# Swin-block kernel: the fifth head's queries and keys come out of the value products, and every engine's order in a step is rewritten

## The chip, the cores and the metric

One core of one Trainium2 chip runs the whole program. The metric is the device time of one execution in microseconds, the median over runs. TensorE does the matmuls, VectorE (DVE) and ScalarE (ACT) empty PSUM and do the elementwise work, GpSimd (POOL) does small side work, and SyncE (SP) issues the DMAs.

## What is computed

```
x2  = relu(x)                                  # 8 images, 16 channels, 56x56
x3  = concat(conv9x9(x2), x2) -> tokens of 160 # DIM = 160
for layer in (0, 1):                           # windows 7x7, layer 1 shifted by 3 and masked
    n   = layernorm(x3);  q,k,v = split(n @ qkvw + qkvb)     # 5 heads of 32
    a   = softmax(q @ k.T * 32**-0.5 + bias (+ mask)) @ v
    x3  = x3 + a @ projw + projb
    x3  = x3 + gelu(layernorm(x3) @ w1 + b1) @ w2 + b2       # MLP = 640
y   = x3 @ linw + linb
out = conv1x1(concat(conv9x9_transposed(y), y)) + convb
```

## The kernel before

Three phases follow each other: the first convolution (phase_a), the two Swin layers (phase_b) and the last convolutions (phase_c). The change is in phase_b alone, which works in strips of two window rows: 16 windows, 784 tokens, held as 7 tiles of 112 tokens. There are 32 strips in each of the two layers, so 64 strips.

phase_b is software-pipelined. One body handles three strips at once: the attention of strip i (`la`), the MLP of strip i-1 (`lm`), and the front of strip i+1 (`ln`): turning its normalised tokens and making Q, K and V from them. All engines run an order written out by hand, once in each engine's `body`, and meet by semaphores. A body in which all three are present is called steady. A steady body leaves out waits that the order makes unnecessary.

The names used below. Attention works on four groups j = 0..3 of four windows (two side by side, in both window rows), and the MLP and the products on two halves `HALF` of 4 and 3 tiles.

- T1 (`front_turned`): transposes of z1, the normalised input, into z1t; ACT copies them (`front_hi`) and DVE subtracts the rounded part (`front_lo`). A product of split operands is four matmuls (`split_passes`, L147).
- Q0, K0, B0 and Q1, K1, B1 (`front_product`): queries and keys of heads 0 to 3 for half a strip, 128 weight columns against 400 token columns, and B: queries and keys of the fifth head, 64 weight columns against the same 400.
- V0 to V3 (`values`): values of group j; here the tokens (114) are the stationary side and the 160 weight columns stream.
- `scores(j)`, `weights_turned(j)`, `outputs(j)`, OTj (`outputs_turned`), P0 to P2 (`projection`): attention of group j. Scores and outputs work on 64x64 tiles of the array; each is 20 fp32 matmuls that the trace shows as 40 records. The scores of two row groups go to two PSUM banks.
- T2 (`mlp_turned`), G0 to G9 (`mlp_in`), W0 to W5 (`mlp_out`; W0 has two token tiles, the others one): the MLP. L0 to L3 (`linear`): in layer 1's bodies only.

PSUM banks are shared in rotations. `RA` is a list of uses that take the three banks `ra` in turn, so its order must be the order in which TensorE fills them. `G_USES`, `L_USES` and `W_USES` name the bank of each MLP use; slot 2 is the bank `pt_ps` of the turned weights. `a_freed`, `a_room` and `m_freed` give the semaphore value at which a bank is empty.

The normalisation of a strip's input is `xa_stats` (DVE), `inv_std` (POOL), `xa_normalised` (DVE) and `repeat_rest` (POOL). SP loads the next strip into xa when `xa_normalised` is done. In the kernel before, body i does both `xa_stats(i+2)` and `xa_normalised(i+2)`, and TensorE turns the result a body later.

Of the kernel before, what the change touches and what calls it, by code (L numbers as in the profile page):

```python
# [31 lines left out]
CR = 3 * REST  # L32
# [21 lines left out]
QN = 16 * WQ  # L54
FT = MLP // 128
# [671 lines left out]
def phase_b(nc, keep, late, xs0, xs1, ys):  # L727
    with ExitStack() as ctx:
# [6 lines left out]
        def bank(name):  # L735
# [24 lines left out]
        q4, k4 = sb("q4", [128, QN]), sb("k4", [128, QN])  # L760
# [29 lines left out]
        FRONT = ["T1A0", "T1C0", "T1A1", "T1C1", "Q0", "K0", "B0", "V0", "V1", "Q1", "B1", "K1", "V2", "V3", "OT0"]  # L790
# [6 lines left out]
        T2_USES = [("T2A0", 0), ("T2C0", 1)]  # L797
        G_USES = [(f"G{g}", n) for g, n in enumerate((2, 1, 0, 2, 1, 0, 1, 2, 0, 1))]
        L_USES = [("L0", 2), ("L1", 0), ("L2", 1), ("L3", 2)]
        W_USES = [(f"W{n}", n % 2) for n in range(len(PAIRS))]  # L800
# [180 lines left out]
        def _(pool):  # L981
# [29 lines left out]
            gp.memset(q4[:], 0.0)  # L1011
# [17 lines left out]
            def body(i, la, lm, ln, more=True):  # L1029
                m = i - 1  # L1030

                def front_rest(n):
                    inv_std(n)
                    pool.wait_ge(s_norm[0], n + 1)
                    repeat_rest(z1, s_z[0])

                if lm is None and la is None:
                    front_rest(0)
                if lm is None and la is None:
                    gp.memset(vb[:], 1.0)  # L1040
                    for t in pr:
                        gp.memset(t[:], 0.0)
                    gp.tensor_copy(view(gather, 0, QP, 0, [[WT, 2], [1, WT]]),
                                   view(keep.ident, 0, QP, 0, [[WP, 2], [1, WT]]))
                    gp.tensor_copy(gather[:, GK:QP], keep.ident[0:QP, WT:WP]).then_inc(s_clear, 1)
                if more:
                    front_rest(i + 2)
# [25 lines left out]
        def _(act):  # L1073
            act_ = nc.scalar.activation

            def body(i, la, lm, ln, more=True):
                m = i - 1

                def front_hi(hf):
                    t0, nt = HALF[hf]  # L1080
                    for part, dst, rows in (("A", z1t[0], 128), ("C", z1t[2], CR)):
                        use = f"T1{part}{hf}"
                        act.wait_ge(*a_full(i, use))
                        act_(view(dst, 0, rows, t0 * WIN, [[WIN, nt], [WP, 16], [1, WIN]]),
                             view(bank_a(i, use), 0, rows, 0, [[TT, nt], [WIN, 16], [1, WIN]]), ACT.Copy).then_inc(s_hi1, 1)
# [14 lines left out]
                def fifth_head(hf):  # L1100
                    use = f"B{hf}"
                    act.wait_ge(*a_full(i, use))
                    dims = [[2 * WQ, 4], [1, WT]]
# [7 lines left out]
                def values(j, n):  # L1111
                    use = f"V{j}"
                    act.wait_ge(*a_full(n, use))
                    act_(view(vb, 0, QP, j * VJ, [[VW, 2 * HEADS], [1, HD]]),
                         view(bank_a(n, use), 0, QP, 0, [[HD, 2 * HEADS], [1, HD]]), ACT.Copy).then_inc(a_freed(n, use)[0], 1)
# [37 lines left out]
                if la is not None:  # L1153
                    weights_out(1, i)
                    values(3, m)
# [16 lines left out]
                if ln is not None:  # L1172
                    front_hi(0)
                if la is not None:
                    outputs_hi(1)
                    exps(2, i)
                if ln is not None:
                    front_hi(1)
                if la is not None:
# [8 lines left out]
                if ln is not None:  # L1188
                    values(0, i)
                    values(1, i)  # L1190
                if la is not None:
# [5 lines left out]
                if ln is not None:  # L1197
                    weights_out(0, i + 1)
                    exps(1, i + 1)
                    queries(1)  # L1200
                    fifth_head(1)
                    keys(1)
                    values(2, i)
# [5 lines left out]
        def _(dve):  # L1209
# [43 lines left out]
            def body(i, la, lm, ln, more=True):  # L1253
# [151 lines left out]
                if lm is not None:  # L1405
                    t_lo(1)
                if la is not None:
                    outputs_lo(0)
                if la is not None:
# [13 lines left out]
                if ln is not None:  # L1423
                    front_lo(1)
                if la is None and lm is None:
                    xa_stats(1)
                if lm is not None:
                    mlp_out(0)
                if more:
                    xa_normalised(i + 2)  # L1430
                if lm is not None:
                    mlp_out(1)
                    mlp_out(2)
                if la is not None:
                    outputs(2)
                if ln is not None:
                    scores_biased(0, i + 1, ln)
                    scores_max(0, i + 1)
                    scores_less_max(0, i + 1)
                if la is not None:  # L1440
                    outputs_lo(2)
                    outputs(3)
                if ln is not None:
                    scores_biased(1, i + 1, ln)
                    scores_max(1, i + 1)
                if la is not None:
                    outputs_lo(3)
                if lm is not None:
# [3 lines left out]
                if lm is not None:  # L1452
                    mlp_out(4)
                if la is not None:
# [7 lines left out]
                    residual(2)  # L1462
                    dve.wait_ge(s_pow, 2 * i + 1)
# [11 lines left out]
        def _(pe):  # L1475
            mm, tr = nc.tensor.matmul, nc.tensor.transpose

            def turn(z, hf, bank_of, room, full, name, freed_already=()):
                t0, nt = HALF[hf]
                for part, f0, rows in (("A", 0, 128), ("C", 128, CR)):  # L1480
# [8 lines left out]
            def body(i, la, lm, ln, more=True):  # L1489
# [16 lines left out]
                def front_turned(hf):  # L1506
                    if hf == 0 and not steady:
                        pe.wait_ge(s_z[0], i + 2)
                    turn(z1, hf, lambda u: bank_a(i, u), lambda u: a_room(i, u), lambda u: a_full(i, u)[0], "T1",
                         ("T1A0",) if steady else ())  # L1510

                def front_product(name, hf):
                    c0, n = {"Q": (0, 128), "K": (128, 128), "B": (256, 2 * HD)}[name]
                    use = f"{name}{hf}"
                    if use == "Q0":
                        pe.wait_ge(*a_freed(i, "T1C1"))
                    if use != "Q0" or not steady:
                        room_a(use)
                    filled_a(use, split_passes(nc, bank_a(i, use)[0:n, 0:QH], *[view(t, 0, t.shape[0], hf * 4 * WP, [[8 * WP, 2], [WP, 4], [1, WQ]])
                                                 for t in z1t],  # L1520
                                               *[w[:, c0:c0 + n] for w in keep.w["qkv", ln]], True))

                def values(j, n, l):
                    use = f"V{j}"
                    reach(pe, *a_room(n, use))
                    wv = [w[:, 2 * DIM:3 * DIM] for w in keep.w["qkv", l]]
                    for w in range(2):
                        c = slice((8 * w + 2 * j) * WP, (8 * w + 2 * j) * WP + QP + 1)
                        last = split_passes(nc, bank_a(n, use)[0:QP + 1, w * DIM:(w + 1) * DIM], *[t[:, c] for t in z1t], *wv, False)
                    last.then_inc(a_full(n, use)[0], 1)  # L1530

                def scores(j, n):
# [13 lines left out]
                    for b in range(HEADS):  # L1546
                        for row in range(2):
# [3 lines left out]
                            for w in range(2):  # L1551
                                c = j // 2 * QH + w * (4 * WQ) + (2 * (j % 2) + p) * WQ
                                q = qm[rows, h % 2 * QN + c:h % 2 * QN + c + WT] if h < 4 else q4[rows, c:c + WT]
                                k = (kt if h < 4 else k4)[rows, c:c + WT]
# [490 lines left out]
```

## Time and profile before

| | |
|---|---|
| median of 3 runs | 2950.62 us (2948.6 to 2956.58) |
| the profiled execution | 2952.52 us, span 2951.0 us, mean granted clock 0.986 |
| TensorE matmul busy | 98% of the span |
| TensorE weight loads busy | 92% |
| VectorE, ScalarE, GpSimd busy | 75%, 58%, 28% |
| DMA | 52 GB/s mean |

Ends of matmuls are modelled and overlap the next one, so a busy TensorE can hide short waits; the start of one block of matmuls to the start of the next shows what a block really took.

### The profile page before, as it was taken

How to read it: one execution, taken by the hardware profiler on the slowest of the kernel's cores; microseconds unless marked ns; L12 is line 12 of the kernel's file. 1: busy time of each engine (PE TensorE's matmuls, PEld its weight loads, DVE VectorE, ACT ScalarE, POOL GpSimd, SP SyncE). 2: the span in 40 equal slices, each digit the busy share in tenths (PEclk: the TensorE clock that was granted, in tenths of full speed). 3: DMA queues.
4: the chain of work that ended last, by engine and by line, in shares of the span. 5: the costliest groups of instructions: out<-in, count | busy, mean ns of one | idle time of the engine just before them, and what ended most of it. 6: DMA issues, size and time to landing. Idle time of an engine off the chain costs nothing. (4 is left out here: it accounts for less than half of the span.)

```text
span 2951.0 us, 94022 instructions
## 1 busy us (share of the span) xinstructions
PE 2883.9 (98%) x39898; PEld 2703.9 (92%) x39898; DVE 2213.6 (75%) x6736; ACT 1721.5 (58%) x4076; POOL 837.1 (28%) x1470
## 2 busy tenths in 40 slices
PE   8979999999999999999999999999999999999799
PEld 6669999999999999999999999999999999999799
DVE  5667777887787777787788878778878878887422
ACT  6446666666666666666656655565656555665321
POOL 8122222222222222222323322232323332332111
PEclk9969999999999999999999999999999999999899
DMA  6321111111111111111112221121111111112374
GB/s 155 128 90 25 40 46 43 46 43 46 43 43 30 42 43 46 43 46 43 46 26 47 58 58 34 33 44 44 42 24 44 44 44 25 42 43 46 65 136 77
DMA packets 210768, 152.23 MB, mean 52 GB/s; under 512 B 15954, under 2 KB 205205, under 8 KB 210331
## 3 DMA queue, kind: packets, MB, share of 16 engines
q1 hardware_dynamic: 207619, 142.41, 21.0%
q8 instruction: 308, 5.05, 0.7%
q10 hardware_dynamic: 1008, 3.44, 0.5%
q0 software_dynamic: 1728, 0.48, 0.2%
q14 instruction: 105, 0.86, 0.1%
HBM read 95.64 MB, written 52.50 MB: 50 GB/s over the span
## 5 line engine op out<-in xcount | busy, mean ns | idle before, releaser
L1627 PE MATMUL rm<-w,ht 128*112 128x160 f32 x4480 | 676.5, 300 | 0.0
L1627 PEld LDWEIGHTS rm<-w,ht 128*112 128x112 f32 x4480 | 619.7, 177 | 11.8
L1051 POOL TENSOR_TENSOR rs<-ln_tmp,mhalf 112x4 f32<-112x4 f32 (+1 forms) x128 | 118.8, 928 | 980.3 <-DVE ln_tmp L1233 980.3
L1148 ACT ACTIVATE ht<-rm 128x336 f32<-128x336 f32 (+1 forms) x448 | 216.6, 490 | 124.6 <-PE rm L147 124.5
L1091 ACT ACTIVATE qm<-ra,qpair 128x400 f32<-128x400 f32 x256 | 138.1, 590 | 214.4 <-PE ra L147 214.4
L1124 ACT ACTIVATE pt<-pt_ps 113x490 f32<-113x490 f32 x256 | 149.4, 584 | 184.7 <-PE pt_ps L1566 184.7
L1005 POOL TENSOR_TENSOR z<-z,one 112x448 f32<-112x448 f32 (+2 forms) x192 | 131.4, 684 | 358.2 <-DVE z L1237 358.2
L1119 ACT ACTIVATE pr<-sm 113x490 f32<-113x490 f32 x256 | 159.5, 623 | 88.4 <-DVE sm L1296 87.7
L1338 DVE TENSOR_TENSOR ot_lo<-ra,ot_hi 128x98 fp32r<-128x98 f32 x512 | 109.1, 255 | 128.1 <-ACT ot_rest L1131 118.0
L1131 ACT ACTIVATE ot_hi<-ra 128x98 fp32r<-128x98 f32 x512 | 102.1, 259 | 141.3 <-PE ra L1601 141.3
L1296 DVE TENSOR_TENSOR sm<-sc,mx 113x490 f32<-113x490 f32 x256 | 177.6, 694 | 6.6
L1588 PEld LDWEIGHTS so<-vb,pt 49*49 49x49 f32 x10240 | 140.8, 122 | 42.0 <-issue 41.9
L999 POOL TENSOR_TENSOR ln_tmp<-st 112x7 f32<-112x7 f32 x192 | 34.4, 207 | 507.8 <-DVE st L1214 507.8
L1282 DVE TENSOR_TENSOR sc<-so,tabs 113x490 f32<-113x490 f32 x256 | 169.9, 664 | 10.8 <-PE so L1555 6.8
L1288 DVE TENSOR_REDUCE mx<-sc 113x10 f32<-113x490 f32 x256 | 169.9, 664 | 8.8
L1566 PE MATMUL pt_ps<-gather,pr 113*128 113x113 f32 x1280 | 174.0, 267 | 0.0
L1555 PE MATMUL so<-kt,qm 64*49 64x49 f32 x8192 | 168.2, 207 | 2.4 <-ACT k L1107 2.4
L1486 PE MATMUL ra<-ident,z 112*128 112x112 f32 (+1 forms) x1280 | 158.1, 263 | 12.4 <-POOL z L1005 10.3
L1588 PE MATMUL so<-vb,pt 49*49 49x33 f32 x10240 | 169.3, 210 | 0.0
L1237 DVE TENSOR_SCALAR z<-x,mean,rs 112x160 f32<-112x160 f32 x448 | 133.8, 359 | 37.5 <-POOL rs L1051 35.4
L147 PE MATMUL rm<-z2t_hi,w_hi 128*128 128x336 f32 (+1 forms) x448 | 159.0, 355 | 0.0
L1486 PEld LDWEIGHTS ra<-ident,z 112*128 112x128 f32 (+1 forms) x1280 | 137.2, 136 | 19.3 <-POOL z L1005 10.7
(276 smaller groups left out, 9231.8 us busy)
## 6 DMA issues: line engine op xcount, KB each, us to landing
xa<-xs SPq DMA_DIRECT2D x128, 245.0 KB
xr<-xs SPq DMA_DIRECT2D x128, 245.0 KB
xs<-xo SPq DMA_DIRECT2D x64, 245.0 KB
ys<-yz SPq DMA_DIRECT2D x64, 245.0 KB
c_y<-ys SPq DMA_DIRECT2D x36, 260.0 KB
xs<-a_tok SPq DMA_DIRECT2D x14, 560.0 KB, 6.1
xs<-tok_late SPq DMA_DIRECT2D x14, 560.0 KB, 6.7
a_nat<-in_x ACTq DMA_DIRECT2D x7, 480.0 KB, 6.2
```

The lines of the kernel that those rows point to most:

```text
L147: last = nc.tensor.matmul(out, lhs, rhs, start=(n == 0), stop=(n == len(pairs) - 1))
L1119: act_(view(pr[j % 2], 0, QP, 0, [[WP, 2 * HEADS], [1, WT]]), view(sm[j % 2], 0, QP, 0, [[WT, 2 * HEADS], [1, WT]]), ACT.Exp).then_inc(s_e ...
L1124: act_(pt[:], pt_ps[0:QP, 0:HEADS * GK], ACT.Copy).then_inc(s_pte, 1)
L1148: act_(ht[:, f * SN + t0 * TT:f * SN + (t0 + nt) * TT], bank_m(i, lm, use)[:, 0:nt * TT], ACT.Gelu_apprx_tanh).then_inc(m_freed(i, lm, use ...
L1282: v.tensor_tensor(view(sc, 0, QP, 0, [[SX, 2], [1, SX]]), view(so, 0, QP, 0, [[512, 2], [1, SX]]), tab, ALU.add).then_inc(s_sadd, 1)
L1288: v.tensor_reduce(mx[:], s3, AX.X, ALU.max).then_inc(s_smax, 1)
L1296: v.tensor_tensor(sm[j % 2][:].rearrange("q (g k) -> q g k", k=WT), s3, view(mx, 0, QP, 0, [[1, 2 * HEADS], [0, WT]]), ALU.subtract).then_ ...
L1486: last = tr(bank_of(use)[0:rows, t * TT:(t + 1) * TT], z[:, c:c + rows], keep.ident[0:TT, 0:TT])
L1555: last = mm(so[w * WP:w * WP + WT, row * 512 + b * WT:row * 512 + (b + 1) * WT], q, k, start=True, stop=True)
L1566: last = tr(pt_ps[:, h * GK:h * GK + QP], pr[j % 2][:, SLOT[h] * 2 * WP:(SLOT[h] + 1) * 2 * WP], gather[:])
L1588: last = mm(so[w * WP:w * WP + WT, p * 512 + OC + h * VW:p * 512 + OC + (h + 1) * VW], pt[p * WP:p * WP + WT, h * GK + w * WT:h * GK + (w ...
L1627: last = mm(bank_m(i, lm, use)[0:TT, t * DIM:(t + 1) * DIM], ht[:, c:c + TT], keep.w["w2", lm][:, f * DIM:(f + 1) * DIM], start=(f == 0), ...
```

## The change

`values` streams 224 weight columns in place of 160: the last 64 columns of the query and key part (the fifth head) and the 160 value columns (`VC`). ScalarE copies the values to `vb` as before, and the 64 columns of each window pair to a new buffer `qk5`. B0 and B1 are no longer products: each is 8 fp32 matmuls on 64x64 tiles that turn `qk5` against the identity (`fifth_head`), alternately on the tile of rows and columns 0 to 63 and on that of rows and columns 64 to 127, all into one PSUM bank. ScalarE takes B in three copies in place of four. q4 and k4 are laid out by group.

The orders change too. V0 and V1 go ahead of Q0, V2 goes ahead of the projection, and V3 moves from the next body's start to stand between Q1 and the end of W4. W0 is split around T1C1 and OT1, and W4 around the projection and Q1. W1 and W2 move behind B0 and behind `weights_turned(3)`. On VectorE `xa_normalised(i+1)` now runs in body i, after `t_lo(1)`, and `xa_stats(i+2)` after `mlp_out(0)`; `outputs(3)` goes ahead of `outputs_lo(2)`, and `mlp_out(4)` behind `residual(2)`. ScalarE and GpSimd follow. The bank rotations are rewritten to fit.

```
+VC = 2 * HD + DIM
+        qk5 = sb("qk5", [QP, 2 * 128])
-        RA = Ring(["T1A0", "T1C0", "OT1", "T1A1", "T1C1", "Q0", "K0", "B0", "V0", "V1", "OT2", "OT3", "P0", "P1", "P2",
-                   "Q1", "B1", "K1", "V2", "V3", "T2A1", "T2C1", "OT0"], 3, {})
+        RA = Ring(["T1A0", "T1C0", "T1A1", "T1C1", "OT1", "V0", "V1", "Q0", "K0", "B0", "OT2", "OT3", "V2", "P0", "P1", "P2",
+                   "Q1", "V3", "B1", "K1", "T2A1", "T2C1", "OT0"], 3, {})
-        G_USES = [(f"G{g}", n) for g, n in enumerate((2, 1, 0, 2, 1, 0, 1, 2, 0, 1))]
+        G_USES = [(f"G{g}", n) for g, n in enumerate((1, 0, 2, 1, 0, 2, 1, 0, 2, 1))]
...
# ScalarE
                 def fifth_head(hf):
-                    for p in range(2):
-                        act_(view(q4, p * WP, HD, hf * QH + p * WQ, dims), view(bank_a(i, use), 0, HD, p * WQ, dims), ACT.Copy,
-                             scale=float(HD) ** -0.5)
-                        last = act_(view(k4, p * WP, HD, hf * QH + p * WQ, dims), view(bank_a(i, use), HD, HD, p * WQ, dims),
-                                    ACT.Copy)
+                    act_(q4[:, cols], bank_a(i, use)[:, 0:2 * GK], ACT.Copy, scale=float(HD) ** -0.5)
+                    for p in range(2):
+                        last = act_(k4[p * WP:p * WP + HD, cols], bank_a(i, use)[p * WP + HD:(p + 1) * WP, 0:2 * GK], ACT.Copy)
+                def values(j):
+                    act_(view(vb, 0, QP, j * VJ, [[HEADS * VW, 2], [VW, HEADS], [1, HD]]),
+                         view(bank_a(i, use), 0, QP, 2 * HD, [[VC, 2], [HD, HEADS], [1, HD]]), ACT.Copy)
+                    act_(view(qk5, 0, QP, j % 2 * 128, [[2 * HD, 2], [1, 2 * HD]]),
+                         view(bank_a(i, use), 0, QP, 0, [[VC, 2], [1, 2 * HD]]), ACT.Copy).then_inc(a_freed(i, use)[0], 1)
...
# VectorE
+                if la is not None and ln is not None:
+                    xa_normalised(i + 1)
                 if la is not None:
                     outputs_lo(0)
...
-                if more and la is not None:
-                    xa_stats(i + 2)
                 if ln is not None:
                     front_lo(0)
+                    front_lo(1)
                 if la is not None:
                     outputs_lo(1)
-                    front_lo(1)
                 if lm is not None:
                     mlp_out(0)
                 if more:
-                    xa_normalised(i + 2)
+                    xa_stats(i + 2)
...
# TensorE
+                def fifth_head(hf):
+                    use = f"B{hf}"
+                    pe.wait_ge(*a_freed(i, f"V{2 * hf + 1}"))
+                    if hf == 1:
+                        room_a(use)
+                    for n in range(4):
+                        for p in range(2):
+                            rows = slice(p * WP, p * WP + WT)
+                            last = mm(bank_a(i, use)[p * WP:(p + 1) * WP, n * WT:(n + 1) * WT], qk5[rows, n * WP:(n + 1) * WP],
+                                      keep.ident[rows, rows], start=True, stop=True)
+                    filled_a(use, last)
...
                 if ln is not None:
+                    values(0)
+                    values(1)
                     front_product("Q", 0)
                     front_product("K", 0)
-                    front_product("B", 0)
-                if lm is not None:
-                    mlp_out(2)
+                    fifth_head(0)
+                if lm is not None:
+                    mlp_out(1)
...
```

## Rows read from the trace of the kernel before

**Rows 1.** The page's busy shares by engine, and the granted TensorE clock by slice.

```profile
PE 2883.9 (98%) x39898; PEld 2703.9 (92%) x39898; DVE 2213.6 (75%) x6736; ACT 1721.5 (58%) x4076; POOL 837.1 (28%) x1470
...
PEclk9969999999999999999999999999999999999899
```

**Rows 2.** TensorE's timeline, T2 at two bodies' starts: start us, us, line, operation, count.

```profile
995.94 0.99 PE L1486 MATMUL rm<-ident,z 112*128 112x112 f32 x8
...
1034.95 0.98 PE L1486 MATMUL rm<-ident,z 112*128 112x112 f32 x8
```

**Rows 3.** TensorE's timeline from W0 to weights_turned(3) in that body.

```profile
1010.05 2.88 PE L1627 MATMUL rm<-w,ht 128*112 128x160 f32 x20
1012.77 0.74 PE L1486 MATMUL ra<-ident,z 112*128 112x112 f32 x6
...
1013.84 1.52 PE L1627 MATMUL rm<-w,ht 128*112 128x160 f32 x10
1015.09 0.46 PE L147 MATMUL ra<-z1t_hi,qkv_hi 128*128 128x400 f32 x1
...
1016.73 0.35 PE L147 MATMUL ra<-z1t_hi,qkv_hi 128*64 128x400 f32 x1
...
1017.48 1.52 PE L1627 MATMUL rm<-w,ht 128*112 128x160 f32 x10
1018.94 0.66 PE L1588 MATMUL so<-vb,pt 49*49 49x33 f32 x40
1019.42 0.23 PE L1555 MATMUL so<-kt,qm 64*49 64x49 f32 x2
...
1020.00 0.71 PE L1566 MATMUL pt_ps<-gather,pr 113*128 113x113 f32 x5
```

**Rows 4.** TensorE's timeline, two value matmuls ten apart.

```profile
1020.82 0.27 PE L147 MATMUL ra<-qkv_rest,z1t_rest 98*114 98x160 f32 x1
...
1021.82 0.26 PE L147 MATMUL ra<-qkv_hi,z1t_lo 128*114 128x160 f32 x1
```

**Rows 5.** The chain that ended last: the last phase's products, 112 weight columns against 224.

```profile
2826.29 16.84 PE c_acc L1963 x162
```

**Rows 6.** TensorE's timeline around W3, OT3, W4, P0, V3 and G0.

```profile
1023.67 1.61 PE L1627 MATMUL rm<-w,ht 128*112 128x160 f32 x10
1025.34 0.61 PE L1601 MATMUL ra<-ident,os 113*128 113x113 f32 x4
...
1026.27 1.52 PE L1627 MATMUL rm<-w,ht 128*112 128x160 f32 x10
1027.60 0.33 PE L147 MATMUL ra<-proj_hi,ot_hi 128*112 128x160 f32 x1
...
1037.40 0.31 PE L147 MATMUL ra<-qkv_hi,z1t_hi 128*114 128x160 f32 x1
...
1038.39 0.44 PE L147 MATMUL pt_ps<-z2t_hi,w_hi 128*128 128x448 f32 x1
```

**Rows 7.** VectorE's timeline: xa_normalised, outputs(3), outputs_lo(3), t_lo(0).

```profile
1015.26 1.99 DVE L1237 TENSOR_SCALAR z<-xa,mean,rs 112x160 f32<-112x160 f32 x7
...
1024.93 0.35 DVE L1313 TENSOR_TENSOR os<-so,rd 113x192 f32<-113x192 f32 x1
...
1027.12 0.42 DVE L1338 TENSOR_TENSOR ot_rest<-ra,ot_rest 32x98 fp32r<-32x98 f32 x2
...
1036.82 0.62 DVE L1350 TENSOR_TENSOR z2t_rest<-rm,z2t_rest 32x448 fp32r<-32x448 f32 x1
```

**Rows 8.** ScalarE's timeline: one copy of fifth_head(0), keys(1), weights_out(1).

```profile
1017.68 0.33 ACT L1105 ACTIVATE q<-ra 32x196 f32<-32x196 f32 x1
...
1034.30 0.51 ACT L1098 ACTIVATE kt<-ra 128x400 f32<-128x400 f32 x1 [0.59 <-PE ra L147]
...
1037.67 0.58 ACT L1124 ACTIVATE pt<-pt_ps 113x490 f32<-113x490 f32 x1 [1.11 <-PE pt_ps L1566]
```

**Rows 9.** Busy time by engine in a window holding one body's loads and store.

```profile
1035.30:1042.30 7.00, 7.00 (x122) 6.39 (x121) 5.86 (x19) 5.59 (x11) 4.69 (x9) 1.00 0.88 215
```

More of the change, by code:

```diff
@@ L1077, in body, with front_hi @@
                 m = i - 1
-                def front_hi(hf):
+                def front_hi(part, hf):
                     t0, nt = HALF[hf]
[L1081 to L1085, printed above, removed]
+                    use = f"T1{part}{hf}"
+                    dst, rows = (z1t[0], 128) if part == "A" else (z1t[2], CR)
+                    act.wait_ge(*a_full(i, use))
+                    act_(view(dst, 0, rows, t0 * WIN, [[WIN, nt], [WP, 16], [1, WIN]]),
+                         view(bank_a(i, use), 0, rows, 0, [[TT, nt], [WIN, 16], [1, WIN]]), ACT.Copy).then_inc(s_hi1, 1)
                 def queries(hf):
@@ L1406, in body @@
                     t_lo(1)
+                if la is not None and ln is not None:
+                    xa_normalised(i + 1)
                 if la is not None:
                     outputs_lo(0)
-                if la is not None:
                     scores_biased(3, i, la)
@@ L1462, in body @@
                     residual(2)
+                if lm is not None:
+                    mlp_out(4)
+                if la is not None:
                     dve.wait_ge(s_pow, 2 * i + 1)
@@ L1476, in _, with turn @@
             mm, tr = nc.tensor.matmul, nc.tensor.transpose
-            def turn(z, hf, bank_of, room, full, name, freed_already=()):
+            def turn(z, hf, bank_of, room, full, name, freed_already=(), parts="AC"):
                 t0, nt = HALF[hf]
-                for part, f0, rows in (("A", 0, 128), ("C", 128, CR)):
+                for part in parts:
+                    f0, rows = (0, 128) if part == "A" else (128, CR)
                     use = f"{name}{part}{hf}"
@@ L1504, in filled_m, with front_turned @@
                     last.then_inc(m_full(i, lm, use)[0], 1)
-                def front_turned(hf):
-                    if hf == 0 and not steady:
+                def front_turned(hf, parts="AC"):
+                    if hf == 0:
                         pe.wait_ge(s_z[0], i + 2)
                     turn(z1, hf, lambda u: bank_a(i, u), lambda u: a_room(i, u), lambda u: a_full(i, u)[0], "T1",
-                         ("T1A0",) if steady else ())
+                         ("T1A0",) if steady else (), parts)
@@ L1516, in front_product, with values @@
+                def values(j):
+                    use = f"V{j}"
+                    if j == 0:
                         pe.wait_ge(*a_freed(i, "T1C1"))
-                    if use != "Q0" or not steady:
+                    elif j > 1:
                         room_a(use)
-                    filled_a(use, split_passes(nc, bank_a(i, use)[0:n, 0:QH], *[view(t, 0, t.shape[0], hf * 4 * WP, [[8 * WP, 2], [WP, 4], [1, WQ]])
-                                                 for t in z1t],
-                                               *[w[:, c0:c0 + n] for w in keep.w["qkv", ln]], True))
@@ L1596, in outputs_turned @@
                     pe.wait_ge(s_od, i * NG + j + 1)
-                    if not steady:
+                    if not steady or j == 1:
                         reach(pe, *a_room(n, use))
@@ L1613, in mlp_in @@
                             pe.wait_ge(*turned_freed(i, lm, f"T2C{hf}"))
-                        if la is not None and g == 0:
+                        if la is not None and g == 2:
                             pe.wait_ge(s_pte, i * NG + 2)
@@ L1679, in body @@
                     front_turned(0)
+                    front_turned(1, "A")
+                if lm is not None:
+                    mlp_out(0, 0, FT)
+                if ln is not None:
+                    front_turned(1, "C")
                 if la is not None:
```

124 lines of the change are left out of this document (60 added, 64 removed).

## The prediction

> **What bounds the kernel now.** I read the page first. The reader should see TensorE at 98% in nearly every slice, at the full clock (2.4 GHz) through the middle phase, with weight loads at 92% and VectorE at 75% [rows 1]. So TensorE is the bound, but its busy share can't say how much is waiting, because modelled ends overlap the next matmul. I therefore took TensorE's timeline of one steady body and measured each block from its first start to the next block's first start. A body runs from T2 to T2: 1034.95 - 995.94 = 39.01 us [rows 2]. Only two things can make the change worth anything: fewer microseconds of matmul in those 39.01, or fewer waits. Both are small, so each is counted, per body, and multiplied by 64 strips. The other engines' timelines are needed for the waits, since several blocks start just after another engine has finished.
>
> **Removed: the products B0 and B1.** B0 lasts from 1016.73 to 1017.48, so 0.75 us for four matmuls [rows 3]. B1 has the same four. Together 1.51 us.
>
> **Added to the value products.** Ten value matmuls start 1.00 us apart: 100 ns each for 114 weight-load columns and 160 streamed columns [rows 4]. The nearest row for 224 streamed columns is in the last phase: 162 in 16.84 us, or 104 ns, with 112 stationary columns [rows 5]. Streaming 160 columns would be quicker than 100 ns if the stream set the pace, so the weight load does, and the wider stream hides behind it but for 4 ns. There are 32 such matmuls in a body: +0.13 us. Bounds: 0 if the load still hides all, and 64/160 of 100 ns each, 40 ns x 32 = 1.28 us, if the stream did set the pace; I take the row of 224, since it is the same type with nearly the same load.
>
> **Added: two blocks of small turns.** Each is 8 fp32 matmuls, hence 16 records, two tiles at a time: 8 rounds. No row has this shape. Outputs and scores are 40 records on four tiles, 10 rounds each. Outputs takes 1019.42 - 1018.94 = 0.48 us, or 48 ns a round, with 49 load columns [rows 3]. The round is the same for 33 and for 49 streamed columns, since scores is longer only by its way out, below. So the load seems to set it, and the loads give a line: 48 ns at 49 columns, 100 ns at 114, which is 0.8 ns a column. 64 columns then cost 60 ns, and 8 rounds 0.48 us. Then the entry and the exit. W2 takes 1.46 us in front of outputs, where ten records are worth 1.36 (twenty take 2.72), so entry costs 0.10. Scores takes 0.58 against outputs' 0.48, so exit costs 0.10, and the block behind it seems some 0.04 long [rows 3]. In sum 0.72 us a block, 1.44 for both. Bounds: 0.62 if a round stays at 48 ns, and 1.20 if the two tiles take turns (16 x 60 ns = 0.96, and 0.24). I take 0.72, nearest to the rows of outputs.
>
> So the replacement is about even: 1.44 + 0.13 - 1.51 = +0.06 us.
>
> The entry and exit have a rule behind them. The Trainium skill, TensorEngine Tiling (Array Packing), Key Properties, says that changing the tiling mode drains TensorE; it gives no price. The trace agrees with it (W2 1.46 against 1.36), and it speaks against this change, which enters the small tiles six times a body where there were four. A reader who took only the page's "up to 2x" of small tiles (Theoretical Speedup) would book a gain here that the rows do not give.
>
> **Waits that go.** (a) V3 starts at 1037.40, its eight matmuls are done at 1038.20, but G0 starts at 1038.39 [rows 6]. It waits for weights_out(1), which ends at 1038.25, because G0 lies in the bank of the turned weights [rows 8]. G0 now has another bank, and G2 takes that one 1.7 us later: -0.19. (b) W3 takes 1025.34 - 1023.67 = 1.67 us against 1.36, because OT3 waits for outputs(3), which ends at 1025.28, just before 1025.34 [rows 6, 7]. outputs(3) now goes ahead of outputs_lo(2), whose four subtractions take some 0.9 us (two are 0.42). It then ends before TensorE is through W3: -0.31. (c) W4 takes 1.33 in front of the projection where W1 took 1.25 in front of Q0 [rows 3, 6]; it waits for outputs_lo(3), ending at 1027.54 [rows 7]: -0.08. Together -0.58.
>
> **Waits that come.** (d) V3 used to stand between weights_turned(1) and G0. Now G0 follows directly, and could start where V3 did, 2.45 us into the body. But it needs t_lo(0), whose second subtraction ended 2.49 into the body [rows 2, 7]. ScalarE will be later as well: fifth_head(1) (three copies of 0.33) and keys(1) (0.51) now stand last [rows 8], with K1 the last block of the body, so the first copy of T2 starts some 0.1 later. Then t_lo(0) ends at 2.60, and from such an end to the first matmul was 1038.39 - 1038.25 = 0.14: G0 at 2.74, +0.29. (e) P0 waits for outputs_lo(3) still. By my walk through VectorE's order (outputs(3), outputs_lo(2), scores_biased(1), then outputs_lo(3) behind ScalarE's copy of OT3) it is ready 0.05 after TensorE gets there: +0.05. Together +0.34.
>
> Queued behind G0 is all of the MLP, so (d) delays each later block by the same amount and nobody else is late. Walking on, these are just covered, and need watching: V0 waits for C1's subtraction, which needs the exp of group 2 behind a table load (0.12 us spare); OT3 (0.26 spare); outputs(0), which waits for keys(1) (under 0.1 spare); S0, which waits for the fifth head's copies (0.7 spare). The four new copies to qk5, less two saved for the fifth head, cost ScalarE under 1 us of a body in which it is 58% busy [rows 1]; V1's copy ends before K0 does.
>
> **Work that only moves.** xa_normalised (1.99 us) [rows 7] runs 7.5 to 9.5 us into the body; outputs_lo(0) and scores 3 shift by about as much, and have nearly 2 us of spare before TensorE asks for OT1. POOL's copy of the repeated columns ends at about 10.5, and T1 starts at about 12.2; were that cover gone, each microsecond would fall on TensorE. xa_stats goes where VectorE waited for W1. SP now issues the load of xa at 9.5 rather than at the body's start; behind that wait in SP's queue are the store and the load of xr, due 25 us later. Loads and store of one body, some 1.5 MB, took 7 us at 215 GB/s [rows 9]; xa's third takes 2 to 4 us, and xa_stats asks for it at about 18. Hidden. Layer 1's bodies add linear(); VectorE's four linear_out end before front_lo(0) is asked for, so the same sum holds.
>
> **Sum.** +0.06 - 0.58 + 0.34 = -0.18 us a body, x 64 = -11.5 us. On the profiled execution: 2952.5 - 11.5 = 2941.0. That execution lies 1.9 us above the median of the runs, which gives 2939.
>
> **Rivals.**
>
> Same time: the new order gives back what it saves. Four waits have under 0.3 us of spare by a walk whose steps are good to about 0.1. If two of them miss by 0.1 each, -0.18 becomes 0: 2951. For it speaks that the walk found so many starts close to their release; against it, that the waits before were of the same kind and only three cost anything.
>
> Larger gain: the turns run at 48 ns a round (-0.20 for both) and half of (d) is hidden (-0.15). Then -0.53 a body, -34 us: 2917. For it: the stream is short and the two tiles have rows of their own. Against: the loads are 64 columns wide.
>
> Slower: the two tiles take turns. Both tiles of a turn write one PSUM bank, where scores and outputs give each row group its own bank, so no row shows two row groups in one bank. Each block then costs 1.20: 2.40 + 0.13 - 1.51 - 0.24 = +0.78 a body, +50 us: 3001. It decides from 0.88 us a block on. Against it: the two tiles write different partitions, and column tiles of scores already share a bank.
> The Trainium skill, TensorEngine Tiling (Array Packing), Gotcha 1: PSUM Pressure, says that different row tiles cannot access the same PSUM bank simultaneously. No run here shows it yet; by that rule this case would come about.
>
> **How the numbers follow.** A measurement of this kernel tells about 0.3%, or 9 us, from no change, which is 0.14 us a body. Forecast 0.52, own range 2925 to 2948; same time 0.18, 2946 to 2960; larger gain 0.20, 2905 to 2925; slower 0.10, 2975 to 3005. Faster by over 0.3% means below 2941.8: two thirds of the forecast's chance and all of the larger gain, 0.34 + 0.20 = 0.54. Within 0.3%: 0.18 of the forecast and 0.12 of the second case, 0.30. Slower: 0.06 and 0.10, 0.16. The range for 8 in 10 leaves out the slower case and a little of both ends: 2911 to 2962.
>
> **What would show it.** In the timeline after: B0 from first turn to W1 at 0.72 us (0.62 the larger gain, 1.20 the slower case); value matmuls 104 ns apart; W3 to OT3 at 1.4; G0 2.7 us after T2, with VectorE as its releaser; a body of 38.8 us, and 41.5 in layer 1. A body of 39.0 with the blocks as above would mean that a just-covered wait has opened, most likely V0, outputs(0) or P0. The prediction is wrong if the streams of 224 cost over 110 ns or if xa arrives late.

## The result, and the profile after

The changed kernel takes 2970.88 us (median of 4 runs, 2968.67 to 2976.03) against 2950.02 us for the kernel before (4 runs). The ratio is 1.0069, 95% interval 1.0049 to 1.0089. It is slower by 21 us, where 2939 us and a gain were forecast. The profiled execution has a span of 2967.1 us.

The page of the kernel after: busy shares by engine, and the clock by slice. They look like those before [rows 1]: TensorE is the bound in both.

```profile
PE 2875.6 (97%) x41434; PEld 2701.9 (91%) x41434; DVE 2246.8 (76%) x6736; ACT 1706.9 (58%) x4204; POOL 838.3 (28%) x1469
...
PEclk9989999999999999999999999999999999999999
```

TensorE's timeline of one layer 0 body after: start us, us, line, operation, count, and in brackets the idle time before it.

```profile
988.35 0.93 PE L1491 MATMUL rm<-ident,z 112*128 112x112 f32 x8
...
990.94 0.47 PE L148 MATMUL rm<-z2t_hi,w_hi 128*128 128x448 f32 x1
...
1005.37 0.34 PE L148 MATMUL ra<-qkv_hi,z1t_hi 128*114 128x224 f32 x1
...
1007.13 0.35 PE L148 MATMUL ra<-z1t_hi,qkv_hi 128*128 128x400 f32 x1
...
1008.75 0.67 PE L1545 MATMUL ra<-ident,qk 49*64 49x49 f32 x16
1009.35 1.61 PE L1647 MATMUL rm<-w,ht 128*112 128x160 f32 x10
1010.89 0.66 PE L1606 MATMUL so<-vb,pt 49*49 49x33 f32 x40
...
1015.40 1.61 PE L1647 MATMUL rm<-w,ht 128*112 128x160 f32 x10
1016.85 0.55 PE L1619 MATMUL ra<-ident,os 113*128 113x113 f32 x4
...
1018.56 0.71 PE L1647 MATMUL rm<-w,ht 128*112 128x160 f32 x4
1019.06 0.33 PE L148 MATMUL ra<-proj_hi,ot_hi 128*112 128x160 f32 x1
...
1027.25 0.93 PE L1491 MATMUL rm<-ident,z 112*128 112x112 f32 x8
```

T2 to T2 is 38.90 us where it was 39.01 [rows 2]: layer 0 is slightly faster, by 0.11 us where 0.18 was forecast. Next, the same view in layer 1 after: T2 at two bodies' starts, 42.66 us apart, and then `linear()` of the second body (L0 to L3, 28 matmuls).

```profile
1967.05 0.93 PE L1491 MATMUL rm<-ident,z 112*128 112x112 f32 x8
...
2009.71 0.93 PE L1491 MATMUL rm<-ident,z 112*128 112x112 f32 x8
...
2021.84 0.24 PE L148 MATMUL rm<-lin_hi,z2t_hi 128*112 128x160 f32 x1
...
2024.08 0.26 PE L148 MATMUL rm<-lin_rest,z2t_rest 96*112 96x160 f32 x1
2025.13 0.33 PE L148 MATMUL rm<-lin_hi,z2t_hi 128*112 128x160 f32 x1 [0.79 <-DVE yz L1331]
...
2025.59 1.23 PE L1491 MATMUL ra<-ident,z 112*128 112x112 f32 x11
```

And of the kernel before, the first matmuls of L0, of L3 and of T1 behind L3.

```profile
2019.46 0.24 PE L147 MATMUL pt_ps<-lin_hi,z2t_hi 128*112 128x160 f32 x1
...
2021.79 0.26 PE L147 MATMUL pt_ps<-lin_hi,z2t_hi 128*112 128x160 f32 x1
...
2022.19 0.95 PE L1486 MATMUL ra<-ident,z 112*128 112x112 f32 x8
```

L takes 2025.59 - 2021.84 = 3.75 us after and 2.73 before. The first matmul of L3 waits, because L3 uses L0's bank and VectorE has not emptied it: `linear_out(0)` is late. The sharing of that bank is not new: before, L3 used L0's bank too (`pt_ps` in both rows), 2.33 us after L0's start. The waits of the kernel after (total us, times, longest) have this wait in 30 bodies; before there is none of the kind.

```profile
PE rm L148 <- DVE yz L1331: 23.6, 30, 0.8
```

Adding up the starts of T2 in both traces shows where the loss lies. The 31 bodies of layer 0 are 3.5 us shorter (0.11 each), the two at the change of layers 0.8 longer, and the 29 of layer 1 27.2 longer (41.73 to 42.66, 0.94 each): +24.5. The two profiled executions differ by less, 16.1 us, because the first body starts 5.3 us earlier after and what follows these bodies is 3.1 shorter. That start moves by about 4 us without a change in the kernel (e11 and e12 below).

**Why `linear_out(0)` is late.** VectorE's timeline after, in that body: the normalisation of xa, then `linear_out(0)` and what stands between.

```profile
2017.41 3.23 DVE L1241 TENSOR_SCALAR z<-xa,mean,rs 112x160 f32<-112x160 f32 x7
2020.67 0.43 DVE L1342 TENSOR_TENSOR ot_lo<-ra,ot_hi 128x98 fp32r<-128x98 f32 x2
...
2024.14 0.35 DVE L1317 TENSOR_TENSOR os<-so,rd 113x192 f32<-113x192 f32 x1
2024.41 0.67 DVE L1331 SCALAR_TENSOR_TENSOR yz<-rm,std,x1b 112x160 f32<-112x160 f32 x2
```

GpSimd's timeline after, `base_second` of layer 1 in two halves, a multiplication and an addition each.

```profile
2013.73 1.25 POOL L1023 TENSOR_TENSOR x1b<-lin_sum,mean 112x640 f32<-112x640 f32 x1
2015.06 1.88 POOL L1026 TENSOR_TENSOR x1b<-x1b,b 112x640 f32<-112x640 f32 x1
2016.90 0.98 POOL L1023 TENSOR_TENSOR x1b<-lin_sum,mean 112x480 f32<-112x480 f32 x1
2017.96 1.21 POOL L1026 TENSOR_TENSOR x1b<-x1b,b 112x480 f32<-112x480 f32 x1
```

The seven instructions of the normalisation take 3.23 us here and 1.99 in a layer 0 body [rows 7]. The first two of them, from the same timeline in narrow windows:

```profile
2017.41 0.58 DVE L1241 TENSOR_SCALAR z<-xa,mean,rs 112x160 f32<-112x160 f32 x1
...
2017.91 1.37 DVE L1241 TENSOR_SCALAR z<-xa,mean,rs 112x160 f32<-112x160 f32 x1
```

The first takes 0.58 us and ends at 2017.99, 0.1 behind the end of GpSimd's multiplication; the second takes 1.37 and ends at 2019.28, 0.1 behind the end of its addition; the other five take 0.35. VectorE queues in order, so all of it comes 1.24 us later, and the normalisation itself now stands ahead of `linear_out` where it stood behind it. Before, these GpSimd operations ran from 2010.47 to 2015.9 with no normalisation beside them.

The Trainium skill, SBUF — State Buffer, section "SBUF: two separate sides", says that VectorE and GpSimd share a port pair as an exclusive lock, held for a whole instruction, which VectorE needs for an operation with two SBUF inputs or in a mode that uses both ports. The trace agrees on the hold: 1.37 us for an instruction of 0.35, ending just behind GpSimd's. The normalisation has one tensor input in SBUF; in which mode it ran, no run here shows.

### The profile page after: what moved, and what is told of

Its sections match the earlier page's. It is cut to its first block and busy times, and to the rows that moved or that the text cites. A ratio compares the mean times of both kernels' runs of the same rounds, so it can differ in the third digit from the quotient of the medians.

```text
span 2967.1 us, 97285 instructions
## 1 busy us (share of the span) xinstructions
PE 2875.6 (97%) x41434; PEld 2701.9 (91%) x41434; DVE 2246.8 (76%) x6736; ACT 1706.9 (58%) x4204; POOL 838.3 (28%) x1469
## 5 line engine op out<-in xcount | busy, mean ns | idle before, releaser
L1647 PE MATMUL rm<-w,ht 128*112 128x160 f32 x4480 | 692.9, 302 | 0.7 <-DVE yz L1331 0.7
L1647 PEld LDWEIGHTS rm<-w,ht 128*112 128x112 f32 x4480 | 610.7, 177 | 7.9 <-DVE yz L1331 1.1
L1152 ACT ACTIVATE ht<-rm 128x448 f32<-128x448 f32 (+1 forms) x448 | 219.4, 504 | 55.8 <-PE rm L148 52.8
L1241 DVE TENSOR_SCALAR z<-xa,mean,rs 112x160 f32<-112x160 f32 x448 | 169.7, 447 | 2.1
L1491 PE MATMUL ra<-ident,z 112*128 112x112 f32 (+1 forms) x1280 | 157.2, 262 | 13.1 <-POOL z L1007 11.6
L148 PE MATMUL rm<-z2t_hi,w_hi 128*128 128x448 f32 (+1 forms) x448 | 167.7, 374 | 1.6 <-DVE z2t_rest L1354 1.6
L148 PE MATMUL rm<-z2t_rest,w_rest 98*128 98x448 f32 (+1 forms) x448 | 156.2, 349 | 0.0
```

The source lines that it names most:

```text
L148: last = nc.tensor.matmul(out, lhs, rhs, start=(n == 0), stop=(n == len(pairs) - 1))
L1152: act_(ht[:, f * SN + t0 * TT:f * SN + (t0 + nt) * TT], bank_m(i, lm, use)[:, 0:nt * TT], ACT.Gelu_apprx_tanh).then_inc(m_freed(i, lm, use ...
L1241: ins = v.tensor_scalar(z[:, t * ZW:t * ZW + DIM], x_[:, t * DIM:(t + 1) * DIM], mean[n][:, t:t + 1], rs[n][:, t:t + 1], ALU.subtract, ALU ...
L1491: last = tr(bank_of(use)[0:rows, t * TT:(t + 1) * TT], z[:, c:c + rows], keep.ident[0:TT, 0:TT])
L1647: last = mm(bank_m(i, lm, use)[0:TT, t * DIM:(t + 1) * DIM], ht[:, c:c + TT], keep.w["w2", lm][:, f * DIM:(f + 1) * DIM], start=(f == 0), ...
```

## The experiments

Theory A: GpSimd's `base_second` holds VectorE's normalisation at its new place, and this alone delays `linear_out(0)`. Theory B: the new place costs it anyway, 2 us of work ahead of `linear_out`. A third possibility was that the turns are what is wrong.

**e1: hardly any base_second.**

```
-                part = view(x1b, 0, TT, t0 * DIM, [[DIM, nt], [1, DIM]])
+                part = view(x1b, 0, TT, t0 * DIM, [[DIM, nt], [1, 4]])
```
(the operands likewise)

> The changed kernel with GpSimd's four instructions of base_second cut from 160 columns to 4 a tile (so x1b is not computed in layer 1; that part of the result is left out). Nothing else moves. Theory A, VectorE's normalisation of xa is held until GpSimd's running instruction ends: the seven instructions of it take 2.0 us in layer 1 in place of 3.2, linear_out(0) starts 1.2 us earlier, L3 no longer waits, a layer 1 body falls from 42.66 to about 41.7 us, layer 0 stays at 38.89, and the whole run is at about 2941 us. Theory B, the new place of the normalisation alone makes L3 wait, whoever else is busy: the body stays at 42.6 us and the run at 2970 us.

Measured 2944.09 us (one run; before, on the same chip, 2949.07). Layer 1 bodies 41.63, L 2.73, and L3 no longer waits for yz; the mean instruction of z<-xa is 366 ns where it was 447. In the kernel after, then in e1 (busy us, mean ns, idle us before):

```profile
L1241 DVE TENSOR_SCALAR z<-xa,mean,rs 112x160 f32<-112x160 f32 x448 | 169.7, 447 | 2.1
```
```profile
L1241 DVE TENSOR_SCALAR z<-xa,mean,rs 112x160 f32<-112x160 f32 x448 | 132.7, 366 | 2.1
```

Without GpSimd's work beside it, the new place costs nothing. Layer 0 stays at 38.90.

**e2: the normalisation later in layer 1**, clear of GpSimd but right ahead of `linear_out(0)`.

```
-                if la is not None and ln is not None:
+                if la is not None and ln is not None and lm != 1:
                     xa_normalised(i + 1)
...
                     outputs(1)
+                if la is not None and ln is not None and lm == 1:
+                    xa_normalised(i + 1)
```

> The changed kernel, but in layer 1 VectorE normalises xa behind outputs(1), just ahead of linear_out(0), when GpSimd has finished base_second; layer 0 as it is. Theory A (held by GpSimd): the seven instructions take 2.0 us, they run where VectorE waits for L0 anyway, L3 does not wait, a layer 1 body is at 41.7 us and the run at about 2941 us, 0.3% under the kernel before. Theory B (the place in front of linear_out is what costs): linear_out(0) is still late by the 2.0 us that stand in front of it, and L3 waits for some 0.5 us or more: a body above 42.2 us, 2956 us or more.

Measured 2961.26 us, ratio to before 1.0043 (1.0026 to 1.0060): only 10 of the 27 us. The numbers are those of theory B. Two rows of VectorE and the wait that stays:

```profile
2019.46 2.00 DVE L1241 TENSOR_SCALAR z<-xa,mean,rs 112x160 f32<-112x160 f32 x7
2021.38 0.67 DVE L1331 SCALAR_TENSOR_TENSOR yz<-rm,std,x1b 112x160 f32<-112x160 f32 x2
```
```profile
PE rm L148 <- DVE yz L1331: 14.0, 30, 0.5
```

The normalisation is not held (2.00 us), but it now fills the gap in which `linear_out(0)` would have run: L 3.42, layer 1 bodies 42.33. At its place in the change it has an idle stretch of VectorE behind it to be absorbed in; here it has none. So place matters too, though it is not what the change got wrong.

**e3: the turns tile by tile**, to see whether two tiles that write one PSUM bank take turns.

```
-                    for n in range(4):
-                        for p in range(2):
+                    for p in range(2):
+                        for n in range(4):
```

> The changed kernel with the two loops of TensorE's fifth_head swapped: four turns on one 64x64 tile, then four on the other, in place of alternating. Theory P, the two tiles work side by side and a record of one tile costs 51 ns: the 16 records go from 0.41 us to about 0.8, B's block from 0.60 to 1.0 us, a body is 0.8 us longer less what the waits take up, and the run 40 to 50 us longer. Theory Q, the two tiles take turns already because they write one bank: swapping changes nothing, 0.60 us and 2971 us.

Measured 3007.17 us (one run). The block of turns and the W behind it, in TensorE's timeline:

```profile
1024.03 0.94 PE L1545 MATMUL ra<-ident,qk 49*64 49x49 f32 x16
1024.90 1.61 PE L1647 MATMUL rm<-w,ht 128*112 128x160 f32 x10
```

0.87 us in place of 0.60: on one tile each record takes 58 ns, and with the tiles alternating a pair does. The two tiles do work side by side on one bank. The block grows by less than eight times 58 ns, because even in this order the tiles overlap: the second tile's first record starts 6 ns behind the first tile's fifth of eight. Twice 0.27 is the 0.53 us by which the bodies grow (38.90 to 39.43), less than the 0.8 expected, and 64 times that is 34 of the 36 us.

**e4: the statistics back at their old places** in the new order (`xa_stats(i+2)` behind `outputs(1)`, `xa_normalised(i+2)` last).

> The changed kernel with xa_stats(i+2), inv_std and xa_normalised(i+2) back at their places of before (statistics ahead of front_lo(0), normalisation after mlp_out(0)); TensorE's and ScalarE's new orders stay. Theory A: L3 does not wait in layer 1 (linear_out(0) starts as L0 is done), but the statistics, 1.6 us, now stand ahead of front_lo(0), which T1C1 and OT1 wait for with 0.2 to 0.8 us of spare: a layer 1 body at 41.7 to 42.0 us, a layer 0 body at 39.0 to 39.5, the run between 2945 and 2965 us. Theory B gives the same for L3; the run tells what the statistics' old place costs the new order.

Measured 2992.10 us (one run), the worst but e3 and 27 us above the range expected. L is back at 2.73, yet other waits take its place:

```profile
PE ra L1620 <- DVE z1t_rest L1267: 15.0, 61, 0.2
PE ra L1492 <- DVE z1t_lo L1267: 13.9, 31, 2.9
```

Layer 0 bodies 39.52, layer 1 bodies 42.61: T1C1 and OT1, which the new order asks for early, wait for `front_lo` behind the statistics. So moving the statistics was needed by the rest of the change, and the wait in L comes with the new place of the normalisation.

**e5: base_second's second half in the next body**, behind `front_rest(i+1)`.

```
+                if lm == 1:
+                    base_second(m, 1, *HALF[1])
...
                         base_second(i, 0, *HALF[0])
-                        base_second(i, 1, *HALF[1])
```

> The changed kernel with GpSimd's base_second of the second half moved behind front_rest in the next body, so that only the first half's two instructions stand ahead of VectorE's normalisation of xa; all arithmetic is kept. Theory A (VectorE is held only while GpSimd's own instruction runs): the first half ends 7.1 us into a layer 1 body and the normalisation starts at 7.5, so it takes 2.0 us, L3 does not wait, a layer 1 body is at 41.65 us, layer 0 at 38.89, the run at 2941 to 2944 us, 0.2 to 0.3% under the kernel before. The second half, 2.2 us, ends by 12.8, just before linear_out(0) asks for it at 13.0; if that is late, the body is at 41.8 to 42.0. Theory B (any work of GpSimd in that stretch slows VectorE): no change, 2965 to 2970 us.

Measured 2957.65 us, ratio to before 1.0024 (1.0015 to 1.0033): only half of what was expected. VectorE, then GpSimd:

```profile
2011.17 2.00 DVE L1242 TENSOR_SCALAR z<-xa,mean,rs 112x160 f32<-112x160 f32 x7
...
2015.50 1.46 DVE L1301 TENSOR_TENSOR sm<-sc,mx 113x490 f32<-113x490 f32 x1
```
```profile
2014.14 0.99 POOL L1023 TENSOR_TENSOR x1b<-lin_sum,mean 112x480 f32<-112x480 f32 x1
2015.21 1.22 POOL L1026 TENSOR_TENSOR x1b<-x1b,b 112x480 f32<-112x480 f32 x1
```

The normalisation is free, but `less_max` (sm, two inputs in SBUF) started 0.29 us behind GpSimd's addition and took 1.46 us in place of 0.67: it could not run before that one's end at 2016.43. The hold was moved, not removed; L 3.30, layer 1 bodies 42.21.

**e6: e5 with the first part of the change undone**: B0 and B1 as products of 64 weight columns, values of 160 columns, B1 ahead of W5.

> As the run before, and the swap of the fifth head undone inside the new order: B0 and B1 are products of 64 weight columns again, the value products stream 160 columns, qk5 is gone, and B1 stands ahead of W5 so that ScalarE's four copies are covered. By the blocks in the changed kernel's trace the turns cost 0.79 and 0.74 us with entry and exit, the wider streams 0.16, and the products cost 1.51: the body should be 0.18 us shorter, 38.71 and 41.47, the run some 11 us faster than the run before, near 2932 us. If the turns are what brings the gain of the new kernel, it is slower instead, by 10 us or more.

Measured 2949.09 us, ratio 0.9997 (0.9988 to 1.0006): 8.6 us below e5, where 11 was expected. The 2932 expected was missed because it was counted from what e5 should have given; e5's hold is in this kernel too (L 3.29, layer 1 bodies 41.99). Layer 0 bodies 38.70, so the new order alone takes 0.31 us off a body and the turns put 0.20 back. By blocks, the turns' kernel spends 0.24 more in 32 value matmuls, 0.07 more in the turns with what stands at their edges, and 0.11 less in two short waits.

**e7: one edit of the order, alone in the kernel before**: `outputs(3)` ahead of `outputs_lo(2)` on VectorE (with the wait for the bank that OT3 then needs).

> The kernel before with one swap on VectorE: outputs(3) ahead of outputs_lo(2) (and a wait for the bank ahead of OT3, which the old order made unnecessary). The sum of the prediction books 0.31 us a body for this: 2931 us. Rival: outputs_lo(3) is still behind scores_max(1) on VectorE and ends when it did, so the projection starts when it did; what OT3 gains, W4 waits again in front of the projection, and the body stays at 38.9 to 39.0 us: 2945 to 2951 us.

Measured 2960.24 us (one run): 10 us slower than before, outside both forecasts. W3 to OT3 falls from 1.66 to 1.45, and OT3 from 0.44 to 0.39, but W4 to P0 rises from 1.34 to 1.75. TensorE, and VectorE's rows that explain it:

```profile
1030.95 0.33 PE L147 MATMUL ra<-proj_hi,ot_hi 128*112 128x160 f32 x1 [0.23 <-DVE ot_rest L1338]
```
```profile
1027.01 0.22 DVE L1306 RECIPROCAL rd<-so 113x10 f32<-113x10 f32 x1 [0.75 <-PE so L1555]
...
1030.47 0.42 DVE L1338 TENSOR_TENSOR ot_rest<-ra,ot_rest 32x98 fp32r<-32x98 f32 x2
```

`outputs_lo(2)` had filled the 0.75 us in which VectorE waits for the scores. Put behind `outputs(3)`, it makes `outputs_lo(3)` late, and P0 waits. In the changed kernel V2 stands ahead of P0 and covers just that: the edit gains only together with V2's move.

**e8: base_second in its clear stretches.** `base_second` is split into `base_times` (the multiplication) and `base_plus` (the addition). The second half's multiplication goes directly behind `power(1)`; its addition stays where e5 has the second half, in the next body.

```
                     power(1)
+                    if la == 1 and lm == 1:
+                        pool.wait_ge(*m_freed(i, lm, "L3"))
+                        base_times(i, 1, *HALF[1])
                     turned_rest(1)
```

> The changed kernel with GpSimd's four base_second operations of layer 1 at other places: the multiplication of the second half (0.98 us) directly behind power(1), ahead of repeat_rest; the first half behind repeat_rest, as in the changed kernel; the addition of the second half (1.21 us) in the next body behind front_rest(i+1). Nothing else changes. In the run with the second half whole in the next body, xa_normalised took its 2.00 us again, but less_max there took 1.46 us and not 0.67 beside GpSimd's 0.99 and 1.22, linear_out(0) came 0.79 us late and L still took 3.30 us in place of 2.73. If VectorE is held only while a GpSimd operation runs beside a two-operand or scalar operation on SBUF (theory A), the multiplication now ends before z<-x starts and the addition before less_max: L 2.73, layer 1 bodies 41.65, and the run is 32 x 0.57 = 18 us below that one: 2939 to 2941. If linear_out's place alone costs the rest (theory B), L stays at 3.0 to 3.3 and the run at 2950 to 2957.

Measured 2940.12 us, ratio 0.9967 (0.9954 to 0.9979), inside theory A's 2939 to 2941. L 2.73, layer 1 bodies 41.63, with all of x1b computed. VectorE in such a body:

```profile
2006.83 2.00 DVE L1251 TENSOR_SCALAR z<-xa,mean,rs 112x160 f32<-112x160 f32 x7
...
2011.16 0.67 DVE L1310 TENSOR_TENSOR sm<-sc,mx 113x490 f32<-113x490 f32 x1
...
2012.60 0.66 DVE L1341 SCALAR_TENSOR_TENSOR yz<-rm,std,x1b 112x160 f32<-112x160 f32 x2
```

**e9: the same placement with the products of e6.**

> The same placement of base_second with the fifth head's turns undone (B0 and B1 as products of their own, 160-column value products, B1 ahead of W5), so the new order and the moved statistics without the first part of the change. The kernel of that kind with the whole second half in the next body measured 2949.1 with L at 3.29 us and layer 1 bodies at 41.98. With L at 2.73: 41.42, and 32 x 0.56 = 18 us less, 2931 (2929 to 2935), below the kernel before by 0.6%. If another wait in VectorE's queue takes the place of the one removed (theory B), 2945 to 2949.

Measured 2940.16 us, ratio 0.9967 (0.9955 to 0.9979): a miss of 9 us. In this order `power(1)` comes 0.8 us later against z<-x, and the multiplication runs beside its instructions. VectorE, then GpSimd:

```profile
2001.63 1.31 DVE L1253 TENSOR_SCALAR z<-x,mean,rs 112x160 f32<-112x160 f32 x3
```
```profile
2001.31 0.99 POOL L1024 TENSOR_TENSOR x1b<-lin_sum,mean 112x480 f32<-112x480 f32 x1
```

1.31 us in place of 0.91, L 2.92, layer 1 bodies 41.61 where 41.42 was expected: 6 of the 9 us. The other 3 lie ahead of the first body.

**e10: e9 with the two multiplications exchanged.** The first half's runs ahead of `power(1)`, the second half's behind `turned_rest(1)`.

```
                     turned_rest(0)
+                    if la == 1 and lm == 1:
+                        pool.wait_ge(*m_freed(i, lm, "L3"))
+                        base_times(i, 0, *HALF[0])
                     power(1)
-                    if la == 1 and lm == 1:
-                        pool.wait_ge(*m_freed(i, lm, "L3"))
-                        base_times(i, 1, *HALF[1])
                     turned_rest(1)
```

> The last kernel's products, new order and split base_second, with GpSimd's multiplication of the first half moved ahead of power(1) (its mean is ready there) and that of the second half behind repeat_rest. In the last kernel the second half's multiplication ran beside the second z<-x of GpSimd's neighbour, which took 1.31 us in place of 0.91, and L still took 2.92 us in place of 2.73. Theory A (GpSimd beside VectorE's SBUF operations is the whole of it): z<-x 0.91, L 2.73, layer 1 bodies 41.42 to 41.45, and 6 us below the last kernel: 2934. Theory B (linear_out's place): layer 1 bodies stay at 41.6 and the run at 2940.

Measured 2931.63 us, ratio 0.9945 (0.9931 to 0.9959): the fastest kernel here, 0.55% below the one before, and 8.5 us below e9. In the profiles it is 9.5 us: 5.0 of them in the bodies, near the 6 expected, and the rest ahead of the first body. L 2.73, and T2 to T2 in layer 1 is 2032.99 - 1991.54 = 41.45:

```profile
1991.54 0.93 PE L1503 MATMUL rm<-ident,z 112*128 112x112 f32 x8
...
2032.99 0.93 PE L1503 MATMUL rm<-ident,z 112*128 112x112 f32 x8
```

**e11 and e12: both kernels once more**, for the first strip. In the profiles, the first T2 stands at different times: 215.8 us before, 210.5 after, 219.1 in e9.

> The kernel before, once more with a profile. In the four profiles so far of kernels with B0 and B1 as products, TensorE's clock was granted at 0.66 to 0.74 between 200 and 210 us, and the first strip, from the first T1 to the first T2, took 59.4 to 62.6 us; in the seven with the turns 1.00 and 56.3 to 58.1. If the kernel decides this (the turns' shorter loads or the order), this run shows 0.65 to 0.75 there and 59 us or more; if it falls by chance from run to run, it may show either.

> The changed kernel, once more with a profile. If the kernel decides the clock of the first strip, 1.00 between 200 and 210 us and 56 to 58 us from the first T1 to the first T2; bodies 38.90 and 42.66 as in its first profile.

Measured 2948.17 and 2973.01 us (one run each). The first T2 stands at 212.2 and 214.5: the two kernels changed sides. Of these shifts of 3.6 and 4.0 us, 2.5 and 3.0 lie ahead of the first T1 (156.4 us before, 153.8 in e11; 154.2 after, 157.2 in e12), in phase_a. The first strip, from the first T1 to the first T2, took 58.3 us in e11 (59.4 before) and 57.3 in e12 (56.3 after). The clock granted between 200 and 210 us was 0.73 before and 0.66 in e11, 1.00 after and in e12; but e10, which has the products, shows 1.00 there too, and still 60.5 us. The windows of 200 to 210 us of e9 and of e10 (length, busy time by engine in the order PE, PEld, DVE, ACT, POOL, then granted clock, DMA share, GB/s):

```profile
200.00:210.00 10.00, 7.45 (x167) 6.63 (x157) 6.64 (x19) 4.11 (x14) 0.81 (x1) 0.66 0.01 2
```
```profile
200.00:210.00 10.00, 7.87 (x156) 7.12 (x147) 9.15 (x26) 4.09 (x13) 0.00 (x0) 1.00 0.01 2
```

So the products do not by themselves make the clock low at this point, a clock of 1.00 there does not make the first strip short, and the start of the first body moves by about 4 us from one execution to another. The bodies repeat: their sum is 2500.15 and 2500.22 us in the two profiles before, 2524.65 and 2524.62 in the two after. What remains open is why the products' kernels take somewhat longer over the first strip in these few profiles.

## Why the prediction was wrong

**The step that failed** is in "Work that only moves": "Layer 1's bodies add linear(); VectorE's four linear_out end before front_lo(0) is asked for, so the same sum holds." It asked the wrong waiter. The four `linear_out` do end in time for `front_lo(0)`, but L3 needs L0's bank 2.3 us after L0 starts, and that was not walked. Nor was the work beside it: xa_normalised was priced at the 1.99 us of a layer 0 body, and in layer 1 its new place is under GpSimd's `base_second`, where it takes 3.23. This gave +0.94 us a body in half of the bodies, where -0.18 was forecast. e1 and e8 show it: without the overlap L is 2.73 again and the runs are 27 and 31 us below the changed kernel.

**The other steps, in layer 0.** Forecast -0.18 a body, measured -0.11:

- The turns: 0.72 us a block was forecast. The block is 0.60; against e6 the products ahead of it take 0.06 more (1.61 and 1.55) and W1 behind it 0.09 more (1.54 and 1.45), so the first costs 0.75. A round of 64 columns is 58 ns (60 forecast). Right to 0.03.
- The value streams: +0.13 forecast, +0.24 measured by blocks (16 in 1.76 us after, 1.65 in e6). 104 ns was forecast, 105 to 106 came, and the first one of a block is longer. This is the term that was sized too low; it makes the swap +0.20 in place of +0.06.
- Waits that go: (a) went, but was 0.15 and not 0.19, since V3's eighth matmul starts at 1038.15 in the kernel before and is worth 0.10. (b) W3 to OT3 is 1.45, where the sum had put 1.36. It is 1.45 in e6 and e7 too, so 0.09 of it is what this block costs behind the small tiles of scores, and no wait. 0.21 went there and 0.06 in OT3, not 0.31. e7 shows that the reason given was incomplete: the gain stands only because V2 moved ahead of P0.
- Waits that come: (d) G0 starts 2.59 us after T2, forecast 2.74, so against the 2.45 of V3 it costs 0.14 and not 0.29: t_lo(0) ends at 2.53 (2.60 forecast) and G0 follows 0.06 later (0.14 forecast). (e) P0 was about right: the four records of W4 ahead of it take 0.50, where 0.43 would do (W1's 1.25 for ten [rows 3], less six at 0.136), so 0.07 in place of 0.05.
- Together the order gives -0.31 (e6), forecast -0.24.

**The rivals.** Neither the same time nor the larger gain came. The slower case came out in sign, but not by its mechanism: e3 shows that the two tiles don't take turns. The Trainium skill, TensorEngine Tiling (Array Packing), Gotcha 1: PSUM Pressure, would have them do so on one bank; the 58 ns a pair against 58 ns a record says otherwise here, for a diagonal pair of tiles. No rival had layer 1's bodies apart from layer 0's, and that was the gap: half of the bodies were never walked.

**Was the change worth it?** Its order is (e10: -18.6 us), once GpSimd's work is moved with it. Its first part, the turns, is not: 0.20 us a body, about 13 us over 64. e8 against e10 shows 8.5 in the medians and 11.6 in the bodies' sum.

## What to carry to other kernels

When work moves on VectorE, look at what GpSimd does at the new place, in every kind of body: an operation with two inputs in SBUF, or a scalar one on SBUF, waited there for the end of GpSimd's in these traces, and is priced by its row at the old place only if that was as clear. When a queue is rewritten, walk each bank's next user in each variant of the loop, not only the next asker of the engine; a body variant that fills half of the time needs its own walk. And a block that fills an engine's gap is not free to go behind what the gap waits for (e7), unless something else covers its reader.

## What was not expected of the hardware

- VectorE's tensor_scalar on SBUF (0.35 us) took 0.58 and 1.37 beside GpSimd's tensor_tensor, and a two-input tensor_tensor 1.46 in place of 0.67, each ending 0.1 to 0.5 us behind the end of GpSimd's operation. Operations that read PSUM (sc, z2t_lo, ot_lo) kept their times beside it, and so did a tensor_reduce on SBUF (mx, 0.66 from 2013.92 in the kernel after, beside the multiplication).
- Two 64x64 tiles on the diagonal that write one PSUM bank work side by side: 58 ns a pair, and 58 ns a record where one tile works alone.
- While the pipeline fills, the granted clock differed between two executions of one kernel: 0.73 and 0.93 between 170 and 185 us, before and in e11. The first body's start moved by about 4 us with no change in the kernel, but most of that lay ahead of the first T1; what the clock has to do with it is not shown.
